# The order of key tiles and the lead of the scores in a causal attention kernel

## The reference, cut to what matters

```python
mask = jnp.triu(jnp.full((s, s), MASK_VAL, dtype=q.dtype), k=1)[None, None]
scores = jnp.einsum('bhqd,bhkd->bhqk', q, k) / sqrt(d_k) + mask
attn = jax.nn.softmax(scores, axis=-1)
out = jnp.einsum('bhqk,bhkd->bhqd', attn, v)
```

## Time and profile before

| | |
|---|---|
| median of 3 runs | 1868.12 us (1865.41 to 1871.2) |
| the profiled execution's own time | 1867.83 us |
| its span in the profile | 1866.1 us |
| TensorE busy in the span | 1625.2 us (87%) |
| ScalarE busy | 961.9 us (52%) |
| VectorE busy | 925.1 us (50%) |
| GpSimd busy | 456.1 us (24%) |
| mean granted TensorE clock | 0.94 |

### The profile page before, as it was taken

The page is one execution under the profiler, slowest core; times in us unless marked ns, Lnnn a source line. Parts: engine busy times, 40 slices in busy tenths (PEclk is TensorE's granted clock), DMA queues, the critical chain, the costliest instruction groups (busy, mean ns, idle before and its releaser), DMA issues. The chain is left out here.

```text
span 1866.1 us, 30950 instructions
## 1 busy us (share of the span) xinstructions
PE 1625.2 (87%) x10275; PEld 1111.0 (60%) x10276; DVE 925.1 (50%) x1795; ACT 961.9 (52%) x1531; POOL 456.1 (24%) x500
## 2 busy tenths in 40 slices
PE   7769999999999957998559999999568987997998
PEld 5632322322322326887448888888457976896887
DVE  6524433442442436777463333333285555655785
ACT  5459999999999944444242222222123334333332
POOL 0001111210211101555442222222153003001574
PEclk9979999999999978999879999999878997998999
DMA  8981405514523028211231111111212010000001
GB/s 270 278 237 34 85 14 88 87 27 72 87 37 62 18 87 286 85 68 46 71 110 51 51 51 51 50 51 49 86 47 91 1 57 1 1 1 4 23 23 46
DMA packets 79647, 134.44 MB, mean 72 GB/s; under 512 B 11632, under 2 KB 46064, under 8 KB 76400
## 3 DMA queue, kind: packets, MB, share of 16 engines
q1 hardware_dynamic: 72504, 112.00, 23.1%
q0 software_dynamic: 7040, 21.08, 3.6%
HBM read 74.76 MB, written 58.27 MB: 71 GB/s over the span
## 5 line engine op out<-in xcount | busy, mean ns | idle before, releaser
L710 ACT ACTIVATE probs<-ps_s 128x1024 f32<-128x1024 f32 (+3 forms) x640 | 513.8, 954 | 37.1 <-PE ps_s L758 34.2
L775 PE MATMUL ps_o<-probs,V 128*17 128x512 f32 (+3 forms) x2560 | 297.4, 536 | 0.3
L698 POOL TENSOR_SCALAR_AFFINE_SELECT probs<-probs 128x512 f32<-128x512 f32 x128 | 86.6, 678 | 465.6 <-ACT probs L710 461.9
L723 DVE COPY weighted<-ps_o 128x512 f32<-128x512 f32 x32 | 22.1, 689 | 254.1 <-PE ps_o L775 254.1
L758 PEld LDWEIGHTS ps_s<-Q_even,K_even 50*128 50x128 f32 x640 | 56.1, 186 | 152.8 <-ACT probs L710 129.7
L1389 DVE COPY slot_hT<-ps_hT 128x512 f32<-128x512 f32 x72 | 49.8, 691 | 195.8 <-PE ps_hT L1432 195.8
L758 PE MATMUL ps_s<-Q_even,K_even 50*128 50x512 f32 (+3 forms) x640 | 127.6, 446 | 19.5 <-DMA Q_even<-shift_parts 11.5
L730 DVE RECIPROCAL inv_denominator<-ps_o 128x512 f32<-128x512 f32 x32 | 107.4, 3357 | 73.9 <-PE ps_o L789 73.9
L758 PEld LDWEIGHTS ps_s<-Q_odd,K_odd 50*128 50x128 f32 x640 | 55.1, 183 | 139.6 <-ACT probs L710 126.4
L1442 PE MATMUL ps_slot_y<-we_out,slot_hT 128*128 x576 | 136.4, 380 | 0.9 <-DVE slot_hT L1389 0.9
L1921 POOL TENSOR_TENSOR h_lo<-h,h_hi 128x512 fp32r<-128x512 f32 x64 | 89.4, 1414 | 183.8 <-DVE h L1967 183.8
(11 more groups left out here) (279 smaller groups left out, 3953.7 us busy)
## 6 DMA issues: line engine op xcount, KB each, us to landing
qk_stacks<-qk_hi SPq DMA_DIRECT2D x64, 256.0 KB, 4.0
slot_rows<-slots_in SPq DMA_DIRECT2D x72, 128.5 KB, 2.1
qk_stacks<-qk_lo SPq DMA_DIRECT2D x32, 256.0 KB, 4.0
Q_odd<-qk_stacks SPq DMA_DIRECT2D x8, 768.0 KB
K_odd<-qk_stacks SPq DMA_DIRECT2D x8, 768.0 KB
Q_even<-qk_stacks SPq DMA_DIRECT2D x6, 768.0 KB
K_even<-qk_stacks SPq DMA_DIRECT2D x6, 768.0 KB
X<-x SPq DMA_DIRECT2D x8, 512.0 KB, 4.4
```

The costliest lines, as they stand in the source:

```text
L698: pool.affine_select(out=block_of, in_=block_of, compare_op=ALU.is_ge, fill=0.0, base=0, pattern=[[0, HG], [1, P]], channel_multiplier=-1) ...
L710: act.activation(probs[:, at % PROB_BUFS, 2 * p:2 * p + 2, off:BT], ps_s[:, s % SCORE_BUFS, :, off:BT], ACT.Exp).then_inc(exp_ok, 1)
L775: last = pe.matmul(ps_o[32 * h:32 * h + DH + 1, q % 2, off:BT], k["V"][:, group, SEQ_TILES * b + t, h, :], probs[:, at % PROB_BUFS, h, off ...
```

## The change

`TILE_LIST` gets another order within each slice, the same on all engines. Slices 1 to 3 take the whole diagonal tile first, then 384, whole, 256, whole, 128, and then the remaining whole tiles. Slice 0 has no other whole tiles and keeps its order. The first and last positions are found by index (`FIRST`, `LAST`) in place of `t == 0`.

On TensorE the loop now goes by weighings. Ahead of the weighing of position `at` stand all score pairs below 2 at + 2 + LEAD, with a lead of six pairs, or five where that position is the 128-wide tile. Before, it was four in these terms. The score function takes one pair in place of two. Spreading stands behind the weighing of the fourth position after a slice's last (`SPREAD_AFTER`), where it was the second. The numbers of buffers stay 3 and 4.

```diff
-    TILE_LIST = [(q, t, max(0, (t - TB * q) * P)) for q in range(SLICES) for t in range(TB * (q + 1))]
+    def tiles_of(q):
+
+        whole = list(range(TB * q))
+        turns = [t for pair in zip(range(TB * q + 1, TB * q + TB), whole) for t in pair] or list(range(1, TB))
+        return [TB * q, *turns, *whole[TB - 1:]]
+
+    TILE_LIST = [(q, t, max(0, (t - TB * q) * P)) for q in range(SLICES) for t in tiles_of(q)]
     NT = len(TILE_LIST)
+    FIRST = [min(g for g, (q, _, _) in enumerate(TILE_LIST) if q == s) for s in range(SLICES)]
     LAST = [max(g for g, (q, _, _) in enumerate(TILE_LIST) if q == s) for s in range(SLICES)]
...
-    LAG = 2
+    LEAD = {0: 6, P: 6, 2 * P: 6, 3 * P: 5}
+    SPREAD_AFTER = 4
...
-                    if t == 0 and n >= 2:
+                    if g == FIRST[q] and n >= 2:
                         pe.wait_ge(norm_ok, 3 * (n - 2) + 1)
...
-                for at in range(len(STEPS) + LAG + 2):
+                scored = 0
+                for at in range(len(STEPS) + SPREAD_AFTER):
                     if at < len(STEPS):
-                        scores(at)
-                    if 0 <= at - LAG < len(STEPS):
-                        weigh(at - LAG)
-                    if at - LAG - 2 >= 0:
-                        u, g = STEPS[at - LAG - 2]
+                        for s in range(scored, min(2 * at + 2 + LEAD[TILE_LIST[STEPS[at][1]][2]], 2 * len(STEPS))):
+                            scores(s)
+                            scored = s + 1
+                        weigh(at)
+                    if at >= SPREAD_AFTER:
+                        u, g = STEPS[at - SPREAD_AFTER]
                         if g in LAST:
                             spread_denominators(u, LAST.index(g))
```

More of the change, by code:

```diff
@@ L743, in _, with scores @@
                 pe.wait_ge(zero_ok, 1)
-                def scores(at):
+                def scores(s):
+                    at, p = s // 2, s % 2
                     u, g = STEPS[at]
@@ L748, in scores @@
                     q, t, off = TILE_LIST[g]
-                    if g == 0:
+                    if g == 0 and p == 0:
                         pe.wait_ge(loaded[j], 16 * LOADS * (u // 2 + 1))
@@ L752, in scores @@
                             pe.wait_ge(ones_in, 32)
[L753 to L762, removed]
+                    if s >= SCORE_BUFS:
+                        pe.wait_ge(exp_ok, s - SCORE_BUFS + 1)
+                    for h in range(2):
+                        last = pe.matmul(ps_s[:, s % SCORE_BUFS, h, off:BT],
+                                         K[j][HALF * h:HALF * h + USED_ROWS, p, t * P:(t + 1) * P],
+                                         Q[j][HALF * h:HALF * h + USED_ROWS, p, q * BT + off:(q + 1) * BT],
+                                         start=True, stop=True)
+                    last.then_inc(scores_ok, 1)
                 def weigh(at):
@@ L777, in weigh @@
                                          probs[:, at % PROB_BUFS, h, off:BT],
-                                         start=(t == 0), stop=(g == LAST[q]))
+                                         start=(g == FIRST[q]), stop=(g == LAST[q]))
                     last.then_inc(pv_ok, 1)
```

## The result

The changed kernel takes 1888.69 us (median of 4 runs, 1886.62 to 1890.29), the kernel before beside it 1867.12. The ratio is 1.0112 with a 95% interval of 1.0098 to 1.0126. That is 21.6 us slower, above the range of 1864 to 1884; the forecast was +8.5.

The account below looks back on a forecast made before the run. With ScalarE and TensorE both looking full, the order of events was taken to decide. +1 us from order and wait plus 7.5 from clock falls gave +8.5 on 1867.83, 1876.3, stated as 1876.5; range 1864 to 1884.

Parts of the forecast that it names:

- The pauses and ScalarE's bound: ScalarE's timeline: 63.1 us of exponentials in a 68.4 us unit; five pauses with lost overlap explain 4.3 us.
- the 5.3 lost: ScalarE, per unit: 5.3 us beyond its exponentials, 42 us over 8 units, all that a better order can give.
- Part 1, the turns: Slices 1 to 3, narrow tiles alternating with whole ones: slices 2 and 3 lose 0.7 us each instead of about 1.04.
- the turns gain, but little: Slices 2 and 3: small gain, since a whole weighing still precedes scores that the short 128-wide exponentials need soon.
- Part 2, the new wait: TensorE, slice 1's first weighing: waits for the reciprocal in units 1 to 7, costing 2.3 us each.
- The sum without the clock: All units, clock held: -2.0 in unit 0, +1.8 in units 1 to 6, +1.1 in unit 7; sum +1 us.
- Part 3, the clock: TensorE's standstills of about 2.3 us make its clock fall to 0.50, adding 7.5 us.
- seven waits with five falls: TensorE, units 1 to 7: five of the seven new waits bring a clock fall, 7.5 us in all.
- 1.5 us a fall: TensorE at clock 0.50: price of each fall, estimated from the stretch behind 852.39, which loses 1.3 without its ends.
- The counts of six: TensorE's earlier trace: six pauses of 1.3 to 1.7 us kept the clock; of six of 1.8 to 2.9, five lost it.
- Rival (d): TensorE: every wait brings a fall, late scores in following positions another pause; 1880 to 1885 us, chance 0.14.
- the row of 2.49 us without a fall: TensorE's earlier trace: the one pause of 1.8 to 2.9 us without a fall, cited for the clock holding.

Follow-up runs that it names:

- e11: e8 with 256-wide tile second, 128 fourth, 384 sixth in slices 1 to 3, 256 before 384 in slice 0, spreading after 6, 4, 4, 4 positions: 1839.56 us.
- e3: Changed kernel, spread denominators copied out of PSUM before the reciprocal, first weighing waiting for the copy, slice 0's spreading after six positions: 1853.4 us.
- e8: e3 with all leads back to four pairs and spreading after 6, 5, 5 and 4 positions: 1845.97 us.
- e1: Changed kernel with the next pair's scores computed seven times in the wait before slice 1's first weighing: 1869.67 us.
- e5: Kernel before with only the changed order of tiles; lead four pairs and spreading after two positions stay: 1873.74 us.
- e7: Kernel before with spreading alone moved two positions later: 1886.13 us.
- e2: Changed kernel with the reciprocal over only the first 256 of 512 columns: 1855.23 us.
- e9: Changed kernel with the reciprocal over only 384 of 512 columns: 1869.79 us.
- e4: Changed kernel with spreading back after the second position; new order and lead stay: 1872.56 us.
- e6: Kernel before with only the longer lead of six or five pairs; order and spreading as before: 1872.09 us.

## Why the prediction was wrong in size

**The pauses and ScalarE's bound: right.** No unit of any run came below the 63.1 us of exponentials, and of the 5.3 lost e11 gets 68.4 - 65.2 = 3.2 back.

**Part 1, the turns: right in their pauses.** Those of 0.40 and 0.85 measured 0.43 and 0.87. That the gain is small while spreading is at fault is shown by e3 and e8, where it becomes large; "the turns gain, but little" holds only beside whole weighings in the wrong place, as e11 shows.

**Part 2, the new wait: right.** Seven waits of 2.3 us were forecast and measured. The sum without the clock was a little low. e1 shows it, as its phase without its one fall is 554.3 - 2.95 = 551.4 us: +4.0 against before, where the forecast had +1. Of these 3 us, 1.7 are seven units of 68.94 instead of 68.7, and 0.3 is the stray pause; what makes these up I did not pursue. The last 1 us lies ahead of slice 1 of the second unit, where the clock is at 0.50 for 3 us more than before; that this is the cause is not shown.

**Part 3, the clock: the step that failed.** The prediction took "seven waits with five falls", each at "1.5 us a fall". There were seven falls, and six of them lasted 6.8 us, twice the one of the earlier trace rows. Each unit of the changed kernel against e1's without a fall gives the price: the six long falls cost 2.3 to 2.7 us each, 15.1 together, and the short one of unit 1 cost 1.3. So the term was 16.4 us, not 7.5. The phases say the same: 567.8 - 551.4 = 16.4. The price of a short fall was right (1.5 for 1.3, and 1.5 again in e5); two falls too few made 3 us of the error, and the length of the falls made 6. Together with the 4.0 of part 2 the falls give the phase's +20.4 us, from 547.4 to 567.8. The remaining 2 us of the span's 22.4 lie ahead of the phase or behind it. I take them for chance, as the part behind it varies by 8 us with the same code; no run shows that for these 2 us.

The trace before already held a long fall. It is one of the five that the prediction counted, after the pause of 2.91 us that ends here:

```profile
1563.94 0.48 PE L134 MATMUL ps_x<-ident,xn 128*128 128x128 f32 x1 [2.91 <-DVE xn L218]
```

The clock was at 0.50 from 1563.2 to 1570.0, 6.8 us, and fell before TensorE resumed. I had priced all five by the one behind 852.39, of 3.4 us. The counts of six also leave out two pauses with another standstill close behind them, of 1.99 us (to 676.43) and of 1.68 us (to 1401.84); the clock fell in that second standstill, so they show neither case clearly.

Why were most falls long? Not because of the narrow tiles ahead of the wait alone: e7 has them too, with the same wait each time, and four of its seven falls are short. What goes with the length is where the fall begins. In the changed kernel, e2, e7 and e9 there are eighteen falls at these waits. All eleven that began while TensorE stood lasted 6.8 us or more, and all seven that began after it had resumed lasted 3.4. It is no rule without exception: two of e5's falls and e1's only one began behind the standstill and lasted 6.8 us, and the fall in the pause before 1727.54 of the kernel before lasted 3.4. Why the clock falls at one place and not at another with the same wait stays open.

Rival (d), "every wait brings a fall", is what happened, at a chance of 0.14 that was too low: the row of 2.49 us without a fall had too much weight. Its 1880 to 1885 was too low as well, as it priced the falls like the forecast did.

By the Trainium skill ("TensorE: Matmul & The Clock Gate", section "Why this matters for your kernels") all these standstills are short enough to keep the clock. The changed kernel speaks against it seven times in seven, and e9 three times in seven at 1.5 us; e4's seven of 1.2 us agree with it. e1 bears out the page's advice in kind, that TensorE be kept from idling.

## What to carry to other kernels

A shared buffer's release is part of the schedule: when a step is moved later to give one engine room, count forward from it to the next writer of its buffer. A standstill of the engine that feeds the bound one costs its length, and can cost the clock as well: at 2.3 us it did so seven times in seven, at 1.2 us (e4) never. A copy of 0.7 us, so that a buffer comes free before a slow operation, was worth 35 us here, with slice 0's spreading moved to fit. Where two parts of a change are opposed, the sum tells nothing of either: the turns, which looked like a small gain, were worth about 20 us once nothing stood against them.

## What the runs showed of the hardware that was not expected

- TensorE's granted clock fell from 1.00 to 0.50 about 1 us into a standstill of 2.3 us (unit 2 of the changed kernel), and stayed there through 5.5 us of renewed work.
- The same wait of 1.5 us behind the same instructions brought the fall in three units and not in four (e9).
- The same wait of 2.6 us brought falls of 3.4, 6.8 and 10.2 us (e7).
- Two falls of 3.4 us came with no standstill as long as 0.5 us near them (e6).
- Seven repeated pairs of matmuls in a wait, 1.9 us of work without use, took away six of seven falls and 13.5 us of the phase (e1).
